# A four-layer graph network on one Trainium2 core: edge loads by pairs of chunks, waits placed on the DMAs, and a third PSUM bank for turned rows in two passes

## The reference

```python
def _egnn_conv(x, src, dst, edge_attr, W_msg, W_edge, W_root, b):      # layer 0, twice
    msg = x[src] @ W_msg + edge_attr @ W_edge
    agg = jax.ops.segment_max(msg, dst, num_segments=x.shape[0])
    return agg + x @ W_root + b                                        # then leaky_relu
# layer 1
h = relu(edge_attr @ W1.T + b1); w = h @ W2.T + b2
agg = segment_sum(w * x[src], dst); relu(x @ Ws.T + bs + agg @ Wn.T + bn)
# layer 2: two hops of h = segment_sum(norm[:, None] * h[src], dst)
# layer 3: agg = segment_sum(feat_n[src], dst); (agg @ weight) * in_deg ** -0.5 + bias
```

## Time and profile before

| | |
|---|---|
| median of 3 runs | 5183.52 us (5161.65 to 5195.9) |
| profiled execution, its own time | 5204.43 us |
| its span, first to last instruction | 5202.6 us, mean granted PE clock 0.779 of full |
| busy in the span | PE 4056.0 us (78%), POOL 2575.3 (50%), DVE 2241.0 (43%), ACT 1003.2 (19%) |

### The profile page before, as it was taken

How to read it: one execution, slowest core, us unless ns; L and a number is a source line. 1 busy time by engine, 2 the same in 40 slices (tenths; PEclk the granted TensorE clock), 3 DMA queues, 4 the chain that set the end, 5 groups by cost and what they waited for, 6 DMA issues and landing times.

```text
span 5202.6 us, 57278 instructions
## 1 busy us (share of the span) xinstructions
PE 4056.0 (78%) x19316; PEld 2651.9 (51%) x19316; DVE 2241.0 (43%) x5877; ACT 1003.2 (19%) x2108; POOL 2575.3 (50%) x2689
## 2 busy tenths in 40 slices
PE   5776767767356868767765997877897769999999
PEld 4333333333333333333333664544564449999999
DVE  3455554545134544544443555454455452223211
ACT  1100000001112222222222333233233230001111
POOL 4666666664566666666655555555555530000000
PEclk9999999999966565665655556566656659999999
DMA  4333333333233444444432333333333327777776
GB/s 128 96 99 97 93 100 90 100 90 94 47 98 120 137 122 135 127 131 120 137 97 59 113 116 116 116 114 109 108 118 115 117 84 251 268 270 266 263 261 219
DMA packets 261989, 694.99 MB, mean 134 GB/s; under 512 B 83518, under 2 KB 166142, under 8 KB 237950
## 3 DMA queue, kind: packets, MB, share of 16 engines
q1 hardware_dynamic: 66626, 348.21, 19.7%
q0 software_dynamic: 85568, 131.83, 12.8%
q10 hardware_dynamic: 109564, 212.08, 10.9%
HBM read 477.81 MB, written 214.09 MB: 133 GB/s over the span
## 4 chain that ended last, share of the span: by engine, by line
PE 51%; another core or an unknown queue 25%; DVE 13%; issue 6%; ACT 2%; POOL 1%; DMA 1%; DVEq 0%; ACTq 0%; POOLq 0%; SPq 0%
PE banks L1101 17%; PE banks L965 7%; PE banks L1006 6%; DVE scan L1814 5%; PE banks L941 5%; PE banks L961 5%; PE banks L932 5%; PE banks L979 4%; DVE hot_lo L1467 3%; DVE hot_key L1831 2%; DVE hot_hi L1469 1%; DVE hot_src L1833 1%; PE banks L720 1%; ACT adj L1334 1%
## 5 line engine op out<-in xcount | busy, mean ns | idle before, releaser
L694 POOL DMA_INDIRECT gath<-table,ids x2496 | 2399.6, 961 | 1519.6 <-issue 757.8
L1814 DVE TENSOR_TENSOR_SCAN scan<-keep,scan,banks 96x512 f32<-96x512 bf16 x621 | 791.3, 1274 | 1837.7 <-remote 1232.5
L1101 PE MATMUL banks<-r_parts,adj_in 128*128 128x288 bf16 x7203 | 890.4, 286 | 4.9 <-issue 2.5
L979 PEld LDWEIGHTS banks<-ident,scan 96*128 96x128 f32 x2496 | 399.7, 223 | 962.9 <-DVE scan L1814 526.7
L1101 PEld LDWEIGHTS banks<-r_parts,adj_in 128*128 128x128 bf16 x7203 | 883.2, 142 | 7.3 <-DVE r_parts L1515 3.1
L979 PE MATMUL banks<-ident,scan 96*128 96x96 f32 x2496 | 528.6, 359 | 370.3 <-DVE scan L1814 341.6
L965 PE MATMUL banks<-ea,w_edge 32*96 32x512 f32 x832 | 772.7, 1020 | 22.6 <-issue 22.1
L1006 PE MATMUL banks<-hot_key,hot_src 128*128 128x392 bf16 x1600 | 549.1, 478 | 286.6 <-issue 163.0
L1316 ACT ACTIVATE back<-banks 128x384 f32<-128x384 f32 x624 | 305.0, 489 | 2201.2 <-remote 1094.4
L1831 DVE TENSOR_SCALAR hot_key<-iota_key,key_t 128x392 bf16<-128x392 int16 x1600 | 516.7, 323 | 20.7 <-ACT key_t L1355 20.7
L941 PEld LDWEIGHTS banks<-w_edge_out,hid 97*128 97x128 f32 x1664 | 312.4, 281 | 316.2 <-issue 316.2
(11 more groups left out here) (158 smaller groups left out, 2109.2 us busy)
## 6 DMA issues: line engine op xcount, KB each, us to landing
adj_in<-adjacency SPq DMA_DIRECT2D x147, 1568.0 KB
scanned_rows<-back ACTq DMA_DIRECT2D x153, 768.0 KB
adjacency<-adj ACTq DMA_DIRECT2D x100, 784.0 KB
ea<-in_ea_t SPq DMA_DIRECT2D x156, 256.0 KB
gath<-table,ids POOLq DMA_INDIRECT x2496
keep<-keep_max_d SPq DMA_DIRECT2D x104, 384.0 KB
keep<-keep_sum_d SPq DMA_DIRECT2D x52, 384.0 KB
table<-x_sb SPq DMA_DIRECT2D x10, 240.0 KB, 4.3
```

Of the source, the lines that this page charges most:

```text
L694: pool.indirect_dma_start(gath[:, b, t, :], None, tables[p][:, :], bass.IndirectOffsetOnAxis(ap=ids[:, 1, n:n + 1], axis=0),).then_inc(s_g ...
L979: m = pe.transpose(back_ps[g8 % 2][:, t * D:(t + 1) * D], scan[0:D, b, Q * g + t:Q * (g + 1):QT], ident[0:D, 0:D])
L1101: m = pe.matmul(sum_ps[:, u, j, :], adj_in[:, a, :, h], r_parts[:, n % 2, h, :, :].rearrange("p k f -> p (k f)"), start=h == 0, stop=h == ...
L1814: ve.tensor_tensor_scan(scan[0:D, b, at:at + Q], keep[:, b, at:at + Q], turn_ps[k % 2], start, keep_op, take_op).then_inc(s_scan, 1)
```

## The change

- **Loads by pairs.** `ea_of` holds two pairs: pair i lies on 64 partitions, its first chunk on 32 of them and the second on the next 32; `keep_of` likewise holds two pairs along its free axis. SP issues one load of each per pair, 512 KB and 768 KB, once pair i - 2 is done. The edge weights stand in four copies (`w_edge_of`), one for each group of 32 partitions, which SP loads in 12 small DMAs ahead of pass 0.
- **Waits at the DMAs.** `sem_inc(s_passed, 1)` is gone from the loads and the gathers, so the wait is carried by the DMA instruction itself.
- **Three banks and a lag of three in pass 0 and 1.** Turned rows go to banks 4, 5, 2 (pass 0) or 4, 5, 6 (pass 1); turn(k) waits for scan(k - 3), and step k holds turn_back(k - 3). Pass 2 keeps two and two.
- **Counting without a lag in pass 0.** DVE makes the one-hots of quarter k + 1 ahead of scan(k); PE counts quarter k ahead of turn(k). The key lines, which use bank 2 too, wait for scan 6, and turn(8) for their copies.

```diff
 LAG = 2
+LAGS, TURN_BANKS = (3, 3, 2), ((4, 5, 2), (4, 5, 6), (4, 5))
...
+        def edge_columns(i, k):
+            c = DE32 * (2 * (i % 2) + k // 4)
+            return ea_of[c:c + DE32, k % 4 * Q:k % 4 * Q + Q], lambda n: w_edge_of[c:c + DE32, n, :]
+        def pair_loaded(p, i):
+            return PAIRS // 2 * p + i // 2 + 1
+        def turn_at(p, i, k):
+            return banks[0:D, TURN_BANKS[p][(8 * i + k) % len(TURN_BANKS[p])], :]
...
+                for n, w in enumerate((w_l0_edge1, w_l0_edge2, w_edge_in)):
+                    for c in range(4):
+                        sp.dma_start(w_edge_of[DE32 * c:DE32 * (c + 1), n, :], w).then_inc(s_w_edge, 16)
...
-                        for b in (0, 1):
-                            q = 8 * i + 4 * b
-                            at = bass.ds(CHUNK * (2 * i + b), CHUNK)
-                            if not first:
...
-                                    sp.wait_ge(s_turn, QUARTERS * p + q - 4)
-                                sp.sem_inc(s_passed, 1)
-                            sp.dma_start(ea[0:DE32, b, :], ea_t[:, at]).then_inc(s_ea[b], 16)
...
+                        h, at = i % 2, 2 * CHUNK * i
+                        if i > 1:
...
+                                sp.wait_ge(s_turn, QUARTERS * p + 8 * (i - 1))
+                        sp.dma_start(ea_of[2 * DE32 * h:2 * DE32 * (h + 1), :],
+                                     ea_t[:, at:at + 2 * CHUNK].rearrange("f (b e) -> b f e", b=2)).then_inc(s_ea[h], 16)
+                        if i > 1:
+                            sp.wait_ge(s_scan, QUARTERS * p + 8 * (i - 1))
...
+                        sp.dma_start(keep_of[:, h, :], keep_d[0:1, at:at + 2 * CHUNK].to_broadcast([D, 2 * CHUNK]))\
+                          .then_inc(s_keep[h], 16)
...
-                                pool.sem_inc(s_passed, 1)
...
-                        if not under(i, k, 2):
-                            pe.wait_ge(s_scan, base + 8 * i + k - 1)
+                        banks_used = len(TURN_BANKS[p])
+                        if not under(i, k, banks_used):
+                            pe.wait_ge(s_scan, base + 8 * i + k - banks_used + 1)
+                        if p == 0 and i == 1 and k == 0:
+                            pe.wait_ge(s_lines, KEY_BLOCKS)
...
-                        pe.wait_ge(s_hot, 8 * i + k - 1)
+                        pe.wait_ge(s_hot, 8 * i + k + 1)
...
+                            if p == 0 and not (last and k == 7):
+                                one_hots(i + (k + 1) // 8, (k + 1) % 8)
                             scan_quarter(i, k, first)
-                            if p == 0:
-                                one_hots(i, k, first)
```

More of the change, by code:

```diff
@@ L198, in gnn_kernel @@
             with ExitStack() as of_general:
+                ea = sb("ea", [P, 2, CHUNK], at=of_general)
+                keep = sb("keep", [D, 2, CHUNK], BF16, of_general)
                 parts = sb("parts", [P, 2, CHUNK], BF16, of_general)
@@ L215, in gnn_kernel @@
             with ExitStack() as of_fast:
+                ea_of = sb("ea_of", [P, CHUNK], at=of_fast)
+                w_edge_of = sb("w_edge_of", [P, 3, D], at=of_fast)
+                keep_of = sb("keep_of", [D, 2, 2 * CHUNK], BF16, of_fast)
                 key_t = sb("key_t", [P, 2, KEY_TILES, NT * WINDOWS], at=of_fast)
@@ L964, in turn @@
                         if KIND[p] == EDGE32:
[L965 to L966 removed]
+                            columns, weights = edge_columns(i, k)
+                            m = pe.matmul(turn_at(p, i, k), weights(p), columns, start=False, stop=True,
+                                          skip_group_check=True)
                         m.then_inc(s_turn, 1)
                     def turn_back(i, k, first):
[L971 removed]
+                        if first and k < LAGS[p]:
                             return
[L973 removed]
+                        g8 = (k - LAGS[p]) % 8
                         b, g = g8 // 4, g8 % 4
[L975 to L977 removed]
+                        pe.wait_ge(s_scan, base + 8 * i + k - LAGS[p] + 1)
+                        if not (first and k < LAGS[p] + 2):
+                            pe.wait_ge(s_evac, base + 8 * i + k - LAGS[p] - 1)
                         for t in range(QT):
@@ L991, in count @@
                                 m = pe.matmul(hists_ps[s], hot_lo[:, h, s, t, :], hot_hi[:, h, s, t, :],
-                                              start=first and k == 2 and t == 0, stop=last and k == 1 and t == QT - 1,
+                                              start=first and k == 0 and t == 0, stop=last and k == 7 and t == QT - 1,
                                               skip_group_check=True)
@@ L1050, in pair @@
                             turn_back(i, k, first)
-                            count(i, k, first, False)
+                            count(i, k, first, last)
                             if not (first and k == 0) and not (last and k > 0):
@@ L1054, in pair @@
                             turn(i, k)
+                    if p == 1:
+                        pe.wait_ge(s_key_t, SETS)
                     all_pairs(pair, turn_lines if p == 0 else None)
-                    for k in range(LAG):
-                        count(PAIRS, k, False, True)
+                    for k in range(LAGS[p]):
                         turn_back(PAIRS, k, False)
@@ L1813, in scan_quarter, with one_hots @@
                         ve.wait_ge(s_turn, base + 8 * i + k + 1)
-                        ve.tensor_tensor_scan(scan[0:D, b, at:at + Q], keep[:, b, at:at + Q], turn_ps[k % 2],
+                        ve.tensor_tensor_scan(scan[0:D, b, at:at + Q], keep_of[:, i % 2, CHUNK * b + at:CHUNK * b + at + Q], turn_at(p, i, k),
                                               start, keep_op, take_op).then_inc(s_scan, 1)
-                    def one_hots(i, k, first):
-                        if not (first and k < 2):
+                    def one_hots(i, k):
+                        if not under(i, k, 2):
                             ve.wait_ge(s_hist, 8 * i + k - 1)
```

62 lines of the change are left out of this document (27 added, 35 removed).

## The result

| | before | after |
|---|---|---|
| median | 5186.6 us (4 runs, 5161.65 to 5195.9) | 5117.09 us (4 runs, 5102.48 to 5122.14) |
| ratio to before | 1 | 0.9869, 95% interval 0.9829 to 0.9909 |
| span of the profiled execution | 5202.6 us | 5100.6 us |

The changed kernel is 1.3% faster. The range held it; the case that I held likeliest, nothing beyond 1%, did not come. The two profiled executions lie further apart (102 us) than the medians (70 us).

What follows compares the result with a forecast made beforehand. POOL's gathers were taken to stop because word from PE comes late. Terms -9 (third bank), -8 (DMA waits), +3 (pair loads), -2 (counting) gave -16 us, so 5183.5 to 5167 us; range 5085 to 5240.

Steps and rivals of the forecast that it cites:

- the case that I held likeliest: Whole kernel: nothing moves by over 1%, within 5132 to 5235 us, 5167 likeliest; chance 0.53.
- launch shortened: POOL's launch at stops, or one more quarter per stop: either alone gives 5104 to 5112 us, both 5033; chance 0.25.
- What bounds the kernel: POOL's gathers: word from PE comes late, `gath` holds 8 quarters, so 16 gathers, then a 3.4 us stop.
- All at once after POOL has run dry: PE's word during gathers: arrives together only once POOL has stopped, 8.9 us after the turn's recorded end.
- Third bank, lag of three: 0 and -9 us: Pass 0: count holds PE at the same scan, 0; pass 1: sometimes a quarter won, -9 us; both 0 to -71.
- Waits at the DMAs: -8 us of 0 to -79: POOL's launch behind 198 stops: 0.04 us saved each, -8 us; bound 0.40 each, 79 us.
- I take the SP row: 0.04 a stop: POOL's launch priced from SP, which starts at once with the same wait instruction: 0.04 us saved a stop.
- Pair loads: +3 us: Larger loads may be late in pass 1 and 2: 0 to +10 us, +3 taken.
- the 83.74 us before the first turn: Start: 12 small weight loads, some 4 us to issue, were to be covered by this time.
- Counting early: -2 us: End of pass 0: one-hots are done before the last scan, so the degrees start earlier, -2 us.
- Bulkier loads hold the gathers: All gathers slowed by larger loads: 82 us lost, 5266 us, told by mean issue above 0.97 us in pass 0; chance 0.14.

Runs made afterwards that it cites:

- waits: Kernel before, only sem_inc(s_passed) taken out of the gathers and SP's two loads; 1.0000 of before on a chip where POOL never stops (4423 us).
- after_inc: Changed kernel with POOL's sem_inc(s_passed, 1) put back ahead of each quarter's gathers; 1.0000 of before, 5195.6 us, on a chip where POOL stops.
- turn_first_again: Changed kernel with PE's turn(k) ahead of count(k) in pass 0 and of the windows in pass 1; 0.9859 of before where POOL stops.
- experiment 5: Changed kernel with PE's turn ahead of the count or windows, run twice; 1.0074 of before where POOL never stops, 0.9859 where it stops.
- ea_by_chunk: Changed kernel with a pair's edge load issued as two DMAs, one for each chunk; 0.9847 of before, 5118.6 us, where POOL stops.
- waits_third: Kernel before, only sem_inc(s_passed) taken out of gathers and SP's loads, on a chip where POOL stops; 0.9889, 5071.8 against 5128.0 us.
- count_quarter: Changed kernel counting one of four tiles in pass 0, 12 fewer PE instructions a quarter; 0.9834 of before, 5115.3 us, where POOL stops.
- two_banks: Changed kernel with two banks and a lag of two in all passes; 1.0034 of before on a chip where POOL never stops.
- changed: Changed kernel as it is, on a chip where POOL never stops; 1.0031 of before, 4441.3 against 4422.8 us.

## Why the prediction came out as it did

The forecast was 16 us of gain and the result 70. That the range of 5085 to 5240 held it is owed to the rival "launch shortened", which the range took in; the sum itself had priced that term at a tenth of what it was worth.

*What bounds the kernel.* Right for the kernel and the sort of chip of the profile: late word from PE, POOL's eight quarters, a loop of gathers and stops. "All at once after POOL has run dry" is too strong. Inside a run word does come, later each time. In the run behind the earlier trace rows, before:

```profile
616.27 2.02 PE L965 MATMUL banks<-ea,w_edge 32*96 32x512 f32 x2
619.14 1.28 DVE L1814 TENSOR_TENSOR_SCAN scan<-keep,scan,banks 96x512 f32<-96x512 bf16 x1 [1.76 <-PE banks L965]
620.29 2.02 PE L965 MATMUL banks<-ea,w_edge 32*96 32x512 f32 x2
...
631.24 1.28 DVE L1814 TENSOR_TENSOR_SCAN scan<-keep,scan,banks 96x512 f32<-96x512 bf16 x1 [9.11 <-remote]
```

The first of these turns ends at 618.29 and its scan starts 0.85 us later, the next ends at 622.31 and its scan starts 8.93 us later. The 35 us that I cited for the first gather of pass 0 stand in no row; `waits` shows them as 35.0. What I could not know is that two of the five chips have no late word and then a kernel of 4423 us, on which this change loses. The view of the waits shows PE moved from one line to the other just as written; in pass 0, before, and after:

```profile
PE banks L979 <- DVE scan L1814: 251.0, 53, 6.3
```

```profile
PE banks L1015 <- DVE hot_hi L1495: 235.1, 60, 5.6
```

*Third bank, lag of three: 0 and -9 us.* Its value holds: `after_inc` leaves 0 ± 12 us for it and all loads together. The reason was half right. The count does hold PE, but with the count out of the way (`turn_first_again`) nothing is won either, and by the view of experiment 5 PE cannot run ahead then.

*Waits at the DMAs: -8 us of 0 to -79.* This is **the step that failed**: "I take the SP row: 0.04 a stop". The launch behind a stop is 0.54 us shorter in pass 2 (0.81 against 0.27 behind DVE's message) and 0.52 in pass 0 (0.69 against 0.17 behind the scan), more even than the 0.40 that I had as the bound, which was the 0.70 less the 0.30 between two gathers. I assumed that the 0.30 stay, and POOL shows 0.17. SP's row was the wrong neighbour: SP launches at once with or without the increment (its load starts at 607.85 with the word in the earlier trace rows, and at 597.13 beside POOL's 597.15 after the change), so it tells nothing about POOL. As I read it, POOL's launch has a part that can be done while it waits and a part that cannot. The rule of the Trainium skill that I had quoted as the rival ("Perfetto Trace Analysis", "DMA Instruction — SWDGE (GPSIMD)": decoded, then pushed to a wait queue) was nearer, and the trace agrees with it in that a gather that waits by itself starts 0.5 us sooner; that these 0.5 us are decoding no run shows. In sum the term measured -77 us (`after_inc` 5195.6, `ea_by_chunk` beside it 5118.6 us) or, alone and on another chip, -56 us (`waits_third`), and my bound was -79. Had I taken the bound, the forecast would have been 5096 us, 21 us below the result; the rival "launch shortened" gave 5104 to 5112, 5 to 13 us below it, with a chance of 0.25.

*Why no more than that.* 0.52 us for each of the 52 stops of pass 0 would be 27 us, and the pass lost 11.5 us of idle time. With the faster restart the rhythm is another: a run ends after 12 gathers, at times with 4 more behind a short stop, and the period per quarter fell by 0.05 us only (5.84 to 5.79). In `waits_third`, with two banks and a lag of two, runs of 16 stay (43 of 54) and pass 0 has 450.5 us of idle time against 478.4, but on different chips. In pass 2 POOL waits for the message 102 times before and 88 after; times 0.54 that makes 48 to 55 us, and 56.9 went (50.5 between `after_inc` and `ea_by_chunk` on one chip). Why the runs are shorter with the short launch and all other edits, and not with the long launch (`after_inc`), without the other edits (`waits_third`) or with fewer count matmuls (`count_quarter`), I have not settled; that it is the third bank was not tested, since `two_banks` never met a stopping chip.

*Pair loads: +3 us.* On the stopping chips nothing can be told from 0. The first load of pass 1 and of pass 2 is late by 16.3 and 18.2 us, more than the 10 that I had allowed, and it costs nothing: I had priced PE's wait as if PE were what the start of a pass waits for, and POOL was. On the free-running chips POOL's idle time in these passes is the same with the change (253.6 and 266.2 us in `changed`) and without (253.5 and 266.1 in `waits`). What pair loads, weight loads and counting cost there, 14.6 us (`two_banks` against `waits`), lies mostly in pass 0 (13.1). The 12 weight loads took 6.7 us to issue and not 4. The loads at the start, which I had covered by "the 83.74 us before the first turn", were covered by the late word alone.

*Counting early: -2 us.* Right. The degrees follow the last scan at once, 1.20 us after its start, where it was 3.61 in the earlier trace rows:

```profile
1281.65 1.28 DVE L1841 TENSOR_TENSOR_SCAN scan<-keep_of,scan,banks 96x512 f32<-96x512 bf16 x1 [2.74 <-PE banks L989]
1282.85 0.18 DVE L1898 COPY deg<-banks 128x50 f32<-128x50 f32 x1
```

*Bulkier loads hold the gathers.* This did not come: the mean gather in pass 0 is 945 ns, as before, under the 0.97 us that was to decide. It is 982 against 978 in pass 1 and 972 against 961 in pass 2, 12 us in all, but `waits_third`, without a pair load, has 984 and 970.

*The best version.* `waits` is as fast as the kernel before where nothing stops (4422 us, 19 us ahead of the changed kernel) and takes 0.989 where it stops, against 0.987 of the changed kernel with overlapping intervals. The two were not timed side by side on a stopping chip, so which of them is ahead there stays open.

## What to carry to other kernels

Let a GpSimd gather carry its own wait: with an instruction between wait and gather these chips launched it 0.66 to 0.81 us after the word, without it 0.14 to 0.27. Price a launch from the engine that does the launching; a neighbour with the same instruction is no measure. And when the trace shows one engine's word late by microseconds, look for matmuls of one group that come singly; and time on more than one chip before tuning against the delay: here three chips of five had it, and an edit worth 1.1% on one of them was worth nothing on two others.

## What was unexpected in the hardware

- The same kernel took 5128 to 5197 us on three chips and 4423 us on two. The clock granted in the first pass is 1.00 on both and a gather lasts 945 ns on both; what differs there is the word from PE, 0.1 us against up to 8.9.
- On the stopping chips PE's increments arrive late, the more so the longer a run of gathers lasts, and the last of them in a burst 2.7 to 3.0 us after POOL has issued the last gather of a run (611.88 to 614.54 after the change, 604.84 to 607.85 in the earlier trace rows), and matmuls of one group come singly, with 1.1 to 1.2 us ahead of some of them. With more PE instructions per quarter POOL stops more often (124 stops against 79). This fits a queue of finished PE instructions that empties slowly while gathers are issued. That it is such a queue, where it lies, and why two chips do not show it was not settled; every timed execution here was recorded, so whether the recording has a part in it is open too.
- ACT's issue of a small weight load took 18.04 to 19.07 us when SP had sent 12 small loads 13 to 20 us earlier and the pair loads behind them, on the free-running chips, and 0.34 us without them.
